# Norm sums on 64 columns, the guess in PSUM, scores as 64-row products, and a new order of work, in a six-layer local-attention kernel

## What is computed

```python
x = x + attention(layernorm(x))          # x is 4 x 512 x 128; dense, 16 heads of 64
x = x + L0_ffn_ref(layernorm(x))         # where L0_ffn_ref is:
for i in range(6):
    x = attn_layer(shift_tokens(x), Wqkv[i], q_scale[i], k_scale[i], Wo[i]) + x
    x = ffn_layer(shift_tokens(x), ln_g[i], ln_b[i], W1[i], b1[i], W2[i], b2[i]) + x

# attn_layer: q and k are l2-normalised per head, scaled, and rotated;
# local_attention: windows of 32 queries see their own 32 keys and the 32 before them
    sim = jnp.einsum('bhwie,bhwje->bhwij', bq, bk2) * QK_SCALE
    attn = jax.nn.softmax(jnp.where(mask, -max, sim), -1)
# ffn_layer: layernorm, 128 -> 2 x 341, a * gelu(gate), 341 -> 128, + b2
```

## Time and profile before

| | us |
|---|---|
| median of 3 runs | 2199.18 (2197.22 to 2202.99) |
| the profiled execution, its own time | 2200.38 |
| its span from first to last instruction | 2198.6 |
| TensorE (PE) busy in the span | 1996.8 (91%) |
| VectorE (DVE) busy | 1782.8 (81%) |
| GpSimd (POOL) busy | 1497.4 (68%) |
| ScalarE (ACT) busy | 1230.5 (56%) |

### The profile page before, as it was taken

How to read it: one execution, slowest core, us unless ns; L and a number is a source line. 1 busy time by engine, 2 the same in 40 slices (tenths; PEclk the granted TensorE clock), 3 DMA queues, 4 the chain that set the end, 5 groups by cost and what they waited for, 6 DMA issues and landing times.

```text
span 2198.6 us, 49870 instructions
## 1 busy us (share of the span) xinstructions
PE 1996.8 (91%) x17862; PEld 1369.4 (62%) x17862; DVE 1782.8 (81%) x3488; ACT 1230.5 (56%) x2446; POOL 1497.4 (68%) x1438
## 2 busy tenths in 40 slices
PE   8999999997789989989889988998989998899987
PEld 5555555554566666666666666666666766667665
DVE  5666667666899888988899988998889988888974
ACT  5666666663446555555555555555556555565543
POOL 3344444335787887777787887878788777877862
PEclk9999999998899999999999999999999999999999
DMA  4000000003445654555545555454555445554451
GB/s 128 6 6 6 1 11 1 6 1 81 111 118 136 141 135 108 125 131 136 135 110 127 130 135 135 119 129 119 136 141 131 121 114 147 138 120 118 112 122 46
DMA packets 247964, 218.51 MB, mean 99 GB/s; under 512 B 58282, under 2 KB 238248, under 8 KB 247592
## 3 DMA queue, kind: packets, MB, share of 16 engines
q1 hardware_dynamic: 247720, 215.33, 40.0%
...
...
## 4 chain that ended last, share of the span: by engine, by line
PE 25%; DVE 19%; issue 10%; DMA 8%; POOL 7%; ACT 5%; SPq 2%; DVEq 0%; ACTq 0%; POOLq 0%
PE bank L1126 6%; PE bank L940 5%; PE bank L1146 5%; DMA TAB<-rotary_dram 4%; DVE SM L995 3%; DVE SM L993 3%; DVE T L961 2%; PE bank L1299 2%; DMA RB<-norms 2%; DVE T L960 2%; PE bank L1065 2%; DMA norms<-RN 2%; DVE PT L1109 2%; DVE RN L998 2%; PE bank L974 2%
## 5 line engine op out<-in xcount | busy, mean ns | idle before, releaser
L940 PE MATMUL bank<-XT,WQK 128*128 128x256 f32 x1520 | 404.1, 410 | 46.5 <-DVE T L961 43.4
L966 POOL TENSOR_TENSOR T<-T 128x512 f32<-128x512 f32 x288 | 366.5, 1288 | 110.1 <-DVE T L961 109.5
L940 PEld LDWEIGHTS bank<-XT,WQK 128*128 128x128 f32 x1520 | 290.7, 200 | 188.6 <-DVE T L961 96.6
L1018 POOL TENSOR_TENSOR T<-T,RB 128x512 f32<-128x512 f32 x288 | 376.6, 1330 | 29.8 <-DMA RB<-norms 29.7
L946 ACT ACTIVATE SQ<-bank 128x512 f32<-128x512 f32 x380 | 227.6, 604 | 299.1 <-PE bank L940 298.3
L1146 PEld LDWEIGHTS bank<-WU,YS 128*128 128x128 f32 x3072 | 350.3, 192 | 36.6 <-issue 36.6
L680 POOL TENSOR_SCALAR PR<-PR,RI 128x512 f32<-128x512 f32 x256 | 174.0, 693 | 292.2 <-DVE RI L569 291.0
L1146 PE MATMUL bank<-WU,YS 128*128 128x128 f32 x3072 | 365.6, 277 | 3.2 <-ACT YS L1134 2.6
L1134 ACT ACTIVATE YS<-bank 128x512 f32<-128x512 f32 x384 | 209.0, 600 | 140.0 <-PE bank L1126 140.0
L488 ACT ACTIVATE PR<-PR,NM 128x512 f32<-128x512 f32 x256 | 183.4, 717 | 165.9 <-DVE NM L564 164.8
L960 DVE TENSOR_TENSOR T<-bank,TAB 128x512 f32<-128x512 f32 x288 | 196.0, 681 | 88.8 <-ACT SQ L946 42.6
...
## 6 DMA issues: line engine op xcount, KB each, us to landing
RB<-norms SPq DMA_DIRECT2D x384, 128.0 KB, 3.2
QP<-T SPq DMA_DIRECT2D x192, 256.0 KB, 5.1
KZ<-T1F SPq DMA_DIRECT2D x192, 128.0 KB, 3.2
KZ<-T SPq DMA_DIRECT2D x192, 128.0 KB, 3.2
...
```

The costliest lines, as they stand in the source:

```text
L940: m = pe.matmul(b[:, ab * HALF:(ab + 1) * HALF], WQK[n % 3][:, i, ab, :], XT[s % 2][:, hf * HALF:(hf + 1) * HALF], start=True, stop=True)
L966: pool.tensor_tensor(t1, t1, T2[i % 2][:, ::-1, :], ALU.add).then_inc(l_rotated.sem, 1)
L1018: pool.tensor_tensor(t1, t1, RB[:, i:i + 1, :].to_broadcast([P, 2, HALF]), ALU.mult).then_inc(l_scaled.sem, 1)
```

## The change

1. **Norms.** `IND` becomes four matrices of 32 columns. `pe_square_sums` puts a quarter of the positions (64) on each group of 32 rows, so the sums stand on 128 rows by 64 columns: 32 products of 64 columns in place of 8 of 256. `SM`, `LG`, `RN` have 64 columns. The guess is written to PSUM (bank 4, columns 256 to 319) and not to `LG`. So `pe_square_sums` and `pe_heads`, which write bank 4, now wait for `l_newton` and not for `l_clamped`. The norms go out in four DMAs of 16 rows and not in one of 128.
2. **Scores.** `KZ` loses its zero halves. A product covers one head, 64 rows and 64 columns: 64 products a tile in place of 32. The even head of a pair goes to bank 2 and the odd one to bank 3. The relayout of the queries takes eight DMAs in place of four; that of the keys stays at eight. `pe_out` picks its weights by the new order of heads.
3. **Bias.** `b2` is loaded as one more row of `W2S`, against a row of ones in `GE[2]`; the last product of `pe_ffn_down` has 114 rows. `pool_ffn_b2` goes.
4. **Buffers.** The ring `T1` has five buffers in place of four, and fronts run one slot further ahead.
5. **Order.** All five slot functions are rewritten. The fold of the table scales moves from POOL to ACT, and the first half of the copy into `XT` (L924) from DVE to ACT. The table load moves from `k + 4` to `k + 6`, and its fold from `k + 4` to `k + 5`. `dve_max` and `dve_shift` of the two halves no longer stand together.
6. In the first part 16 clears of `KZ` become one, and the first front's norms are changed as in 1.

```diff
-        IND = sb('IND', [P, WIN])
+        IND = sb('IND', [P, HG, WIN])
+        QTR = SEQ // 8
...
-        KZ = [sb(f'KZ{i}', [P, PAIRS, 2, WIN + SEQ // 2]) for i in range(2)]
+        KZ = [sb(f'KZ{i}', [P, PAIRS, WIN + SEQ // 2]) for i in range(2)]
...
-        B2A = sb('B2A', [P, DEPTH, E])
...
-        norms = [nc.dram_tensor(f'norms{i}', (P, HALF), F32).ap() for i in range(2)]
+        norms = [nc.dram_tensor(f'norms{i}', (HEADS, HALF), F32).ap() for i in range(2)]
...
 
...
-                        m = pe.matmul(bank[2][j * WIN:(j + 1) * WIN, 0:HALF], IND[:, :], SQF[j][:, ab, :], start=ab == 0, stop=ab == 1, skip_group_check=True)
+                        for q in range(4):
+                            m = pe.matmul(bank[2][q * WIN:(q + 1) * WIN, 0:QTR], IND[:, j, :], SQF[j][:, ab, q * QTR:(q + 1) * QTR], start=ab + j == 0, stop=ab + j == HG, skip_group_check=True)
                 m.then_inc(s_fsum, 1)
 
...
+            T1 = [T1F] + [sbl(f'T1{i}', [P, HG, 2, HALF]) for i in range(1, NT)]
+            XM = T1[1][:, :, :, :].rearrange('p g a c -> p (g a c)').rearrange('p (t e) -> p t e', e=E)
             T2 = [sbl(f'T2{i}', [P, 2, HALF]) for i in range(2)]
...
-            def pool_fold_scale(l, part):
-                fold_scale(l, part).then_inc(l_folded.sem, 1)
+            def act_fold_scale(l, part):
+                hf, kind = divmod(part, 2)
+                cols = slice(hf * HALF, (hf + 1) * HALF)
+                act.wait_ge(s_tb[part], 16 * (l + 1))
+                for ab in range(2):
+                    c = l * 4 + kind * 2 + ab
+                    i = act.activation(TAB[:, kind, :, ab, cols], TAB[:, kind, :, ab, cols], ACT.Copy, scale=QSC[:, c:c + 1])
+                i.then_inc(l_folded.sem, 1)
...
-                pe.wait_ge(f_b2_added.sem, f_b2_added.at(s - BATCH))
-                pe.wait_ge(l_x2_done.sem, l_x2_done.at(2 * hu - 7))
+                pe.wait_ge(f_x_done.sem, f_x_done.at(s - BATCH))
+                pe.wait_ge(l_x2_done.sem, l_x2_done.at(2 * hu - 8))
...
+                act.activation(XT[s % 2][0:DH, c0:c0 + HALF], bank[7][0:DH, 0:HALF], ACT.Copy).then_inc(l_xt_low_kept.sem, 1)
                 act.activation(XT[s % 2][DH:P, c0 + 1:c0 + 1 + HALF], bank[7][DH:P, 0:HALF], ACT.Copy).then_inc(l_xt_high_kept.sem, 1)
-
-            def dve_keep_xt(hu):
-                s, hf = divmod(hu, 2)
-                c0 = hf * HALF
-                dve.wait_ge(l_x_turned.sem, l_x_turned.at(hu))
-                if s >= 2:
-                    dve.wait_ge(l_front_done.sem, l_front_done.at(4 * s - 5))
-                dve.tensor_copy(XT[s % 2][0:DH, c0:c0 + HALF], bank[7][0:DH, 0:HALF]).then_inc(l_xt_low_kept.sem, 1)
...
-                    if f >= 4 and kind:
-                        dve.wait_ge(s_qp, 64 * ((f - 4) // 2 + 1))
-                    elif f >= 4:
-                        dve.wait_ge(s_kz, 128 * ((f - 4) // 2 + 1))
+                    if f >= NT:
+                        dve.wait_ge(s_kz if kind else s_qp, 128 * ((f - NT) // 2 + 1))
...
                 pe.wait_ge(l_squared.sem, l_squared.at(f))
-                pe.wait_ge(l_clamped.sem, l_clamped.at(f - 1))
-                pe.wait_ge(l_heads_kept.sem, l_heads_kept.at(f - 5))
+                pe.wait_ge(l_newton.sem, l_newton.at(f - 1))
+                pe.wait_ge(l_heads_kept.sem, l_heads_kept.at(f - 6))
                 for ab in range(2):
                     for j in range(HG):
-                        m = pe.matmul(bank[4][j * WIN:(j + 1) * WIN, 0:HALF], IND[:, :], SQ[j][:, ab, :], start=ab == 0, stop=ab == 1, skip_group_check=True)
+                        for q in range(4):
+                            m = pe.matmul(bank[4][q * WIN:(q + 1) * WIN, 0:QTR], IND[:, j, :], SQ[j][:, ab, q * QTR:(q + 1) * QTR], start=ab + j == 0, stop=ab + j == HG, skip_group_check=True)
                 m.then_inc(l_sums_done.sem, 1)
 
-            guess = LG[:, :]
+            guess = bank[4][:, HALF:HALF + QTR]
...
-                dve.tensor_scalar(SM[:, :], bank[4][:, 0:HALF], FAR, NORM2_EPS, ALU.min, ALU.max).then_inc(l_clamped.sem, 1)
+                dve.tensor_scalar(SM[:, :], bank[4][:, 0:QTR], FAR, NORM2_EPS, ALU.min, ALU.max).then_inc(l_clamped.sem, 1)
...
+                for q in range(4):
+                    sp.dma_start(norms[f % 2][:, q * QTR:(q + 1) * QTR], RN[q * WIN:q * WIN + HEADS, :]).then_inc(s_rn, 16)
...
                 for pp in range(2):
-                    for ab in range(2):
-                        if kind:
-                            q = QP[hf][ab * DH:(ab + 1) * DH, :, :].rearrange('p (g e) c -> p g e c', e=2)
-                            sp.dma_start(q[:, :, pp, :], T1[f % 4][pp * DH:(pp + 1) * DH, :, ab, :]).then_inc(s_qp, 16)
-                            continue
-                        for e in range(2):
-                            r = ab * DH + e * WIN
-                            kz = KZ[hf][r:r + WIN, :, e, WIN:].rearrange('p (g e) c -> p g e c', e=2)
-                            r = pp * DH + e * WIN
-                            sp.dma_start(kz[:, :, pp, :], T1[f % 4][r:r + WIN, :, ab, :]).then_inc(s_kz, 16)
+                    for e in range(2):
+                        for ab in range(2):
+                            src = T1[f % NT][pp * DH + e * WIN:pp * DH + (e + 1) * WIN, :, ab, :]
+                            r = slice(e * DH + ab * WIN, e * DH + (ab + 1) * WIN)
+                            if kind:
+                                sp.dma_start(QP[hf][r, pp::2, :], src).then_inc(s_qp, 16)
+                            else:
+                                sp.dma_start(KZ[hf][r, pp::2, WIN:], src).then_inc(s_kz, 16)
...
-                pe.wait_ge(l_masked.sem, l_masked.at(g, half))
-                for pl in range(4):
-                    pr = 4 * half + pl
+                pe.wait_ge(l_masked.sem, l_masked.at(g))
+                for pr in range(PAIRS):
                     for w in range(4):
                         q0 = t % 2 * P + w * WIN
-                        o = sbk[w * WIN:(w + 1) * WIN, :].rearrange('p (k h j) -> p h k j', k=2, h=8)
-                        m = pe.matmul(o[:, 2 * pl:2 * pl + 2, :, :], QP[t // 2][:, pr, q0:q0 + WIN], KZ[t // 2][:, pr, :, q0:q0 + GRP].rearrange('p h (k j) -> p h k j', k=2), start=False, stop=pl == 3, skip_group_check=True)
-                m.then_inc(l_scores_done.sem, 1)
+                        for e in range(2):
+                            r = slice(e * DH, (e + 1) * DH)
+                            o = bank[2 + e][w * WIN:(w + 1) * WIN, :].rearrange('p (k h j) -> p h k j', k=2, h=8)
+                            m = pe.matmul(o[:, pr, :, :], QP[t // 2][r, pr, q0:q0 + WIN], KZ[t // 2][r, pr, q0:q0 + GRP].rearrange('p (k j) -> p k j', k=2), start=False, stop=pr == PAIRS - 1, skip_group_check=True)
+                            if pr == PAIRS - 1 and w == 3:
+                                m.then_inc(l_scores_done.sem, 1)
...
-                pe.wait_ge(l_clamped.sem, l_clamped.at(min(g + 4, FRONTS - 1)))
+                pe.wait_ge(l_newton.sem, l_newton.at(min(g + 5, FRONTS - 1)))
...
                 for h in range(HEADS):
-                    lane, i = h % HG, h // HG
+                    e, pr = divmod(h, PAIRS)
+                    lane, i = pr % 2 * 2 + e, pr // 2
                     m = pe.matmul(bank[7][:, 0:E], YS[:, h, :], WU[:, lp * HG + lane, i * E:(i + 1) * E], start=h == 0, stop=h == HEADS - 1)
...
+                sp.dma_start(W2S[FFR[2][1]:DOWN[2], 2, :], b2[l:l + 1, :]).then_inc(s_w2, 16)
...
-            def pool_ffn_b2(s):
-                pool.wait_ge(f_x_done.sem, f_x_done.at(s))
-                xb = X[:, s % BATCH * TPB:s % BATCH * TPB + TPB, :]
-                b2l = B2A[:, s // BATCH:s // BATCH + 1, :].to_broadcast([P, TPB, E])
-                pool.tensor_tensor(xb, xb, b2l, ALU.add).then_inc(f_b2_added.sem, 1)
...
-                    for c, (c0, n) in enumerate(FFR):
+                    for c, n in enumerate(DOWN):
                         i = pe.matmul(bank[6][:, t * E:(t + 1) * E], GE[c][0:n, t * P:(t + 1) * P], W2S[0:n, c, :], start=c == 0, stop=c == len(FFR) - 1)
                 if part:
                     i.then_inc(f_down_done.sem, 1)
...
@@ -1348,9 +1346,6 @@
                 pool.wait_ge(l_x2_done.sem, l_x2_done.at(TOTAL - 1))
                 pool.wait_ge(s_xb, 16)
                 pool.tensor_tensor(XM[:, rows(b), :], XM[:, rows(b), :], X[:, rows(b), :], ALU.add).then_inc(f_rest.sem, 1)
-                pool.wait_ge(f_rest.sem, f_rest.at(0, 0))
-                b2l = B2A[:, DEPTH - 1:DEPTH, :].to_broadcast([P, TPB, E])
-                pool.tensor_tensor(XM[:, rows(b), :], XM[:, rows(b), :], b2l, ALU.add).then_inc(f_rest.sem, 1)
 
...
@@ -1396,176 +1391,173 @@
 
             def pe_slot(k):
                 if step_at(k - 7, LAST - 1):
-                    pe_ffn_up((k - 7) // 4, 0)
-                if new_f(k + 3):
-                    pe_square_sums(k + 3)
-                if step_at(k - 10, LAST - 2):
```

(2 more changed lines are left out.)

365 lines of the change are left out of this document (183 added, 182 removed).

## The result

The changed kernel takes 2099.95 us, the median of four executions (2095.05 to 2105.09), beside 2199.3 for the kernel before on the same chip: a ratio of 0.9547 (95% interval 0.952 to 0.9574). The forecast of 2034 us was 66 us too low; the range of 1975 to 2150 holds the time, and the sign is the forecast one. The profiled execution took 2105.09 us, 5 above the median.

What follows compares the result with a forecast made beforehand. PE and DVE stood nearly level, with PE waiting on DVE twice a slot. PE busy 1355 plus 76 idle gave 1431 us; with 552.9, 4, 44.1 and 1.8 that made 2034 us, range 1975 to 2150.

Steps and rivals of the forecast that it cites:

- 220 ns an operation: Norms on DVE: each Newton operation, with 64 columns and the guess in PSUM, takes 220 ns, 0.88 us a slot.
- DVE 11.7 us a slot: DVE's work in the middle stretch falls from 14.83 to 11.7 us a slot, by shorter norms and a copy gone.
- no wait of DVE on `TAB`: At a layer change, the earlier table load and fold end a stall that made DVE start the products 3.03 us late.
- sums 1.07: Sums of squares on PE: 64 recorded products of 64 columns still take 1.07 us, no change from 16 of 256.
- the waits on DVE and the unnamed one before the heads: PE's idle time before heads and fronts: 133.6 us in the middle stretch, of which 89 us should go.
- The rival in which small products start no closer than today: Scores and sums on PE: a start every 27 ns is an issue limit, 2.7 us a slot more, 2373 us; chance 0.08.
- the price of the scores: Scores on PE: 128 recorded products, eight overlapping, take 1.08 us a tile, 0.87 us less a slot.
- My rival at 13 to 16 ns: Scores on PE gain nothing at that start distance, the rest holds: 2117 us, or some 30 more for sums; chance 0.13.
- The cover that failed: SP's queue: extra issues delay the norms by 1 us, covered by at least ten us because fronts run a slot further ahead.
- the prologue: Stretch before the first scores, 552.9 us: 4 us more, as POOL has two more rotations before the first relayout.
- the 76 of the forecast: PE's idle time left in the middle stretch, in us: 45 for the new wait on masks and 31 other.
- the masks: PE before the next scores: a new wait for ACT to put down two masks, half a microsecond a slot, 45 us.

## Why the forecast was right, and where it was off

**Right.** That DVE, made slow by POOL, was what PE waited for, and that moving the guess ends it. Forecast 220 ns an operation, measured 220 to 224; DVE 11.7 us a slot, measured 12.04; no wait of DVE on `TAB`, none there; sums 1.07, measured 1.10; the waits on DVE and the unnamed one before the heads, 133.6 us, of which I took off two thirds, fell to 14.7 (2.6 + 12.1). Here I was too careful. The rival in which small products start no closer than today (2373 us) is out. The first 32 products of a tile start about 7 ns apart, but for two breaks, and a tile takes 1.48 us for 128. The Trainium skill's page TensorE: Matmul & The Clock Gate, Part 1, spoke for it with the rule that start to start never falls below about 25 ns; for products in different parts of the array the trace disagrees.

**The step that failed** is the price of the scores, "0.87 less". I had seen four products start together and made 128 of it. The first 32 do run at that pace, but for breaks of 29 and 33 ns; then 56 ns pass, and the other 96 start 10 ns apart on average, in stretches of 8.5 and of 17 (medians over the tiles). A tile takes 1.48 us instead of 1.08. That is 0.4 us a slot, 38 us. The busy time of PE is 1381 against a forecast 1355; some 12 us of the 38 came back elsewhere. My rival at 13 to 16 ns had the mechanism; the mean of 10 ns lies between it and the forecast.

The sum also took it that what PE saves on scores comes off the time in full, 83 of the 165 us that it forecast. In the old order the 34 and 35 us that PE saved brought nothing, with and without the guess; in the new order no run has the old scores. The guess alone, on the other hand, takes 117.8 us off the middle stretch, more than the 111.9 of the whole change. So one term was too large and one too small, and that they partly made up for each other in the sum is luck. What the bias, the fifth buffer and the moved folds and copies are worth, no run shows.

**The cover that failed** is SP's. I had written that if it went, `pool_scale` would be late and with it the scores, and costed it at nothing. I had counted issues at the durations of other slots, 0.3 to 0.65 us, and not looked at which issue stands behind which. The keys were moved straight ahead of the norms, and the issue after them takes 7 us. It is worth some 17 us, by the version with the keys on ScalarE's queue, and part of this is the prologue: 9.5 us where I had 4, and 4.1 with the keys issued later.

**Not foreseen** were the pauses of 48.4 us in the sums, with 8.5 more in the out products. No row of the kernel before shows one in the middle of a line's products. I had priced products by columns and none by instructions. The rest of PE's idle time, 52 us, is less than the 76 of the forecast: 22.6 us for the masks, where I had left 45.

**The tail** grew from 44.1 to 50.7 us. Of these 6.6, some 2 are work that the order leaves behind the last scores (46.1 us in the version with wide sums, with a granted clock of 1.00); the rest goes with the clock, 0.88 of 2.4 GHz on average in this stretch of the profiled execution, where twelve products that took 5.41 us before take 8.46.

The sum: 5.5 (prologue) + 6.6 (tail) + 26.3 (work) + 32.8 (idle) = 71 us, the distance from the forecast span of 2032 to 2103.2.
